# Two cross attentions of a four-layer kernel, from passes over pairs of batches to a pipeline over single batches

## The reference

```
# first layer, per batch; n = layernorm(x), c = ctx, all 256 x 256
q = n @ Wq + bq;  k = c @ Wk + bk;  v = c @ Wv + bv
x = x + tanh(g[0]) * softmax(q @ k.T / 16) @ v

# fourth layer, per batch, 16 heads of 16 features
q = elu(n @ Wq + bq) + 1;  k = elu(c @ Wk + bk) + 1;  v = c @ Wv + bv
S   = einsum('bhle,bhld->bhed', k, q)          # 16 x 16 per head
out = einsum('bhme,bhed->bhmd', v, S) / (sum over head of q*k + 1e-6)
x = x + tanh(g[3]) * (out @ Wo + bo)
```

## Time and profile before

| | |
|---|---|
| median of three runs | 3446.64 us |
| profiled execution, its own time | 3447.9 us |
| its span, from first to last instruction | 3446.2 us |
| PE busy | 3111.9 us, 90% |
| DVE busy | 1781.4 us, 52% |
| ACT busy | 1166.4 us, 34% |
| POOL busy | 355.1 us, 10% |
| mean granted clock of PE | 0.94 |

### The profile page before, as it was taken

How to read it: one execution, slowest core, us unless ns; L and a number is a source line. 1 busy time by engine, 2 the same in 40 slices (tenths; PEclk the granted TensorE clock), 3 DMA queues, 4 the chain that set the end, 5 groups by cost and what they waited for, 6 DMA issues and landing times. The chain is left out here.

```text
span 3446.2 us, 58510 instructions
## 1 busy us (share of the span) xinstructions
PE 3111.9 (90%) x21570; PEld 2500.1 (73%) x21571; DVE 1781.4 (52%) x4412; ACT 1166.4 (34%) x2167; POOL 355.1 (10%) x647
## 2 busy tenths in 40 slices
PE   7868999999997998997999979999799987774998
PEld 5755666666665887886888866666588866673998
DVE  4436777777772113774556557777323336651111
ACT  1213555555552112441212204555432222222221
POOL 1101111111100000000000000010001101113111
PEclk9888999999997999998999989999899988866999
DMA  3010000000002441001000000000111100054554
GB/s 108 0 31 1 1 0 0 0 0 0 0 1 74 151 153 45 18 18 47 0 0 0 0 27 1 0 0 0 57 50 49 49 17 0 0 160 141 182 179 132
DMA packets 93088, 145.92 MB, mean 42 GB/s; under 512 B 12878, under 2 KB 74574, under 8 KB 86864
## 3 DMA queue, kind: packets, MB, share of 16 engines
q1 hardware_dynamic: 89600, 136.39, 12.7%
q0 software_dynamic: 3408, 8.46, 0.7%
HBM read 131.18 MB, written 14.56 MB: 42 GB/s over the span
## 5 line engine op out<-in xcount | busy, mean ns | idle before, releaser
L464 DVE TENSOR_REDUCE m0hnm<-banks 128x4 f32<-128x1024 f32 x256 | 313.0, 1223 | 173.4 <-PE banks L392 173.3
L491 ACT ACTIVATE m0hpT<-banks 128x1024 f32<-128x1024 f32 x256 | 262.8, 1027 | 355.8 <-PE banks L405 355.8
L392 PE MATMUL banks<-m0hk,m0hq 32*128 32x256 f32 x2048 | 292.2, 403 | 12.6 <-DVE m0hnm L464 12.2
L405 PE MATMUL banks<-m0hq,m0hk 32*128 32x256 f32 x2048 | 291.6, 401 | 1.1 <-ACT m0hpT L491 1.1
L489 ACT ACTIVATE a2hpT<-banks,a2hlow 128x512 f32<-128x512 f32 x256 | 161.9, 684 | 181.5 <-PE banks L405 181.5
L392 PEld LDWEIGHTS banks<-m0hk,m0hq 32*128 32x128 f32 x2048 | 175.8, 185 | 64.7 <-DVE m0hnm L464 33.4
L464 DVE TENSOR_REDUCE a2hnm<-banks 128x4 f32<-128x1024 f32 x128 | 156.8, 1225 | 95.4 <-PE banks L392 95.1
L405 PEld LDWEIGHTS banks<-m0hq,m0hk 32*128 32x128 f32 x2048 | 177.7, 184 | 2.1 <-issue 1.7
L1579 ACT ACTIVATE E1sg<-banks 128x256 f32<-128x256 f32 x160 | 61.3, 383 | 326.4 <-PE banks L1596 326.4
L1596 PE MATMUL banks<-e1xnT,E1wg 128*128 128x256 f32 x640 | 166.1, 382 | 0.0
L1596 PE MATMUL banks<-e1xnT,E1wu 128*128 128x256 f32 x640 | 165.1, 381 | 0.0
(11 more groups left out here) (399 smaller groups left out, 6318.2 us busy)
## 6 DMA issues: line engine op xcount, KB each, us to landing
E3w<-in_L_ffn_W_dram SPq DMA_DIRECT2D x47, 1024.0 KB, 5.2
E0w<-in_L_ffn_fw_dram SPq DMA_DIRECT2D x64, 512.0 KB, 4.5
E2w<-in_L_ffn_w_dram SPq DMA_DIRECT2D x16, 1024.0 KB, 7.3
slots_x<-E3zeros SPq DMA_DIRECT2D x1, 5070.0 KB, 25.5
E3xin<-slots_x SPq DMA_DIRECT2D x39, 130.0 KB, 2.1
ctx_in<-in_ctx_dram SPq DMA_DIRECT2D x16, 256.0 KB, 4.8
x_all<-in_x_dram SPq DMA_DIRECT2D x16, 256.0 KB, 5.2
A1ctx_in<-in_ctx_dram SPq DMA_DIRECT2D x16, 256.0 KB, 2.7
```

Of the source, the lines that this page charges most:

```text
L392: ins = pe.matmul(self.scores[:, j, tc], self.q[strip(half, j), u, e, c, chunk(tc)], self.k[strip(half, j), u, e, c], start=True, stop=True)
L405: ins = pe.matmul(self.turned[:, j, kc], self.k[strip(half, j), u2, e2, c2, chunk(kc)], self.q[strip(half, j), u2, e2, c2], start=True, st ...
L464: v.tensor_reduce(self.nm[:, e, :, at:at + 33:32].rearrange("p c g -> p g c"), self.scores, AX.X, ALU.max, negate=True).then_inc(self.nm_r ...
L491: ins = a.activation(dst, self.turned, ACT.Exp)
```

## The change

Both stages run over single batches now. A slot `b` does the second half of batch `b` and the first half of batch `n = b + 1`, on the two sets of four banks in turn (`u` for b, `nu` for n); each engine's program names its steps for both in one order. The slots -1, 0 and 1 are written out, slots 2 to 11 run in a loop of five rounds of two (`Fori` leaves out its upper bound, as in `passes`), and slots 12 to 15 are written out behind it.

The layer norm is in a class `BatchFront`. Statistics and normalised rows are made three batches ahead (b + 3), the transposes of the normalised rows two ahead (b + 2). POOL's root and its copy of the context for batch b + 3 wait until PE is done with v of batch n.

- First attention, PE in a slot: q, k, v (n); transposes of `xn` (b + 2); transposes of the probabilities (b); scores (n); product with v (b). DVE: x of b - 1; q (n); reciprocal (b); statistics (b + 3); v (n); normalised rows (b + 3); maximum (n). ACT: k (n); `xnT` (b + 2); `prT` (b); Exp (n).
- Fourth attention, PE in a slot: q (n); product of k and q (b); k (n); product with v (b); v (n); transposes of `on` (b); transposes of `xn` (b + 2); product with Wo (b), now into bank T3. DVE: bias and x of b - 1; q (n); mask (b); statistics (b + 3); k (n); division (b); normalised rows (b + 3); sum of maximum and Exp, and denominator (n). ACT: Relu and Exp (n); `onT` (b); `xnT` (b + 2); v (n).
- The minimum on DVE is replaced by a Relu with scale -1 on ACT, followed by Exp with scale -1.
- The load of Wq and bq counts on a semaphore of its own (`q_in`), so q of the first batch waits for these two alone.

```diff
+def slots(eng, slot):
+    for b in (-1, 0, 1):
+        slot(b, b % 2)
+    with eng.Fori(1, 6) as i:
+        for u in (0, 1):
+            slot(2 * i + u, u)
+    for b in range(12, B):
+        slot(b, b % 2)
+
+class BatchFront:
...
+    def root(self, g, b, u):
+        g.wait_ge(self.mv_rdy, b + 1)
+        g.tensor_tensor(self.rstd[:, u], self.mv[:, u, :, 1], self.env.eps5[:], ALU.add).then_inc(self.var_rdy, 1)
+        g.wait_ge(self.var_rdy, b + 1)
+        g.tensor_tensor(self.rstd[:, u], self.rstd[:, u], self.env.mhalf[:, 0:C], ALU.pow).then_inc(self.rstd_rdy, 1)
+        g.tensor_copy(self.cT[:, u], self.env.ctxT[:, b]).then_inc(self.cT_rdy, 1)
...
 # both stages, POOL
+            def slot(b, u):
+                if live(b + 3):
+                    g.wait_ge(v_mm, b + 2)
+                    fr.root(g, b + 3, 1 - u)
...
 # layer0_attention, PE
+            def slot(b, u):
+                n, nu = b + 1, 1 - u
+                if live(n):
+                    pe.wait_ge(fr.xnT_rdy, n + 1)
+                    product(pe, lambda m: bankB[nu][:, m], lambda k, m: wq[:, k, chunk(m)],
+                            lambda k: fr.xnT[:, nu, k]).then_inc(q_mm, 1)
...
+                if live(b + 2):
+                    if live(b):
+                        pe.wait_ge(v_rdy, b + 1)
+                    fr.turn(pe, b + 2, u)
+                if live(b):
+                    pe.wait_ge(p_rdy, b + 1)
+                    transpose4(pe, bankC[u], pr[:, u], env.ident[:]).then_inc(pT_mm, 1)
+                if live(n):
+                    pe.wait_ge(q_rdy, n + 1)
+                    pe.wait_ge(k_rdy, n + 1)
+                    product(pe, lambda m: bankB[nu][:, m], lambda k, m: qT[:, nu, k, chunk(m)],
+                            lambda k: kT[:, nu, k]).then_inc(s_mm, 1)
+                if live(b):
+                    pe.wait_ge(v_rdy, b + 1)
+                    pe.wait_ge(pT_rdy, b + 1)
+                    pe.wait_ge(o_used, b + 1)
+                    product(pe, lambda m: bankD[u][:, m], lambda k, m: prT[:, u, k, chunk(m)],
+                            lambda k: vt[:, u, k]).then_inc(o_mm, 1)
...
 # layer3_attention, DVE
+            def slot(b, u):
+                n, nu = b + 1, 1 - u
+                if live(b - 1):
+                    add_up(b - 1, nu)
+                if live(n):
+                    v.wait_ge(q_mm, n + 1)
...
+                if live(b):
+                    v.wait_ge(den_rdy, b + 1)
+                    v.wait_ge(o_mm, b + 1)
+                    v.tensor_tensor(on[:, u].rearrange("p c (h k) -> p (c h) k", k=KD),
...
+                if live(b + 3):
+                    fr.normalised(v, b + 3, nu)
+                if live(n):
+                    v.wait_ge(ex_rdy, n + 1)
+                    v.scalar_tensor_tensor(qk[:, nu], qk[:, nu], 0.0, ex[:, nu], ALU.max, ALU.add).then_inc(qk_rdy, 1)
...
 # layer3_attention, ACT
+                if live(n):
+                    a.wait_ge(raw_rdy, n + 1)
+                    a.activation(ex[:, nu], qk[:, nu], ACT.Relu, scale=-1.0).then_inc(neg_rdy, 1)
+                    a.wait_ge(neg_rdy, n + 1)
+                    a.activation(ex[:, nu], ex[:, nu], ACT.Exp, scale=-1.0).then_inc(ex_rdy, 1)
```

More of the change, by code:

```diff
@@ L225, in _ @@
-            passes(g, body)
+            fr.root(g, 0, 0)
+            fr.root(g, 1, 1)
+            def slot(b, u):
+                if live(b + 3):
+                    g.wait_ge(v_mm, b + 2)
+                    fr.root(g, b + 3, 1 - u)
+            slots(g, slot)
         @block.vector
         def _(v):
[L229 to L244, removed]
+            v.sem_inc(o_used, 2)
+            fr.stats(v, 0, 0)
+            fr.stats(v, 1, 1)
+            fr.normalised(v, 0, 0)
+            fr.normalised(v, 1, 1)
+            v.wait_ge(q_in, 32)
+            def add_up(b, u):
+                v.wait_ge(ri_rdy, b + 1)
+                v.wait_ge(o_mm, b + 1)
+                for c in range(C):
+                    last = v.scalar_tensor_tensor(env.x[:, b, c], bankD[u][:, c], ri[:, u, c:c + 1], env.x[:, b, c],
+                                                  ALU.mult, ALU.add)
+                last.then_inc(o_used, 1)
@@ L269, in _ @@
-            passes(v, body)
+                if live(b + 3):
+                    fr.normalised(v, b + 3, nu)
+                if live(n):
+                    v.wait_ge(s_mm, n + 1)
+                    v.tensor_reduce(nm[:, nu, :], bankB[nu], AX.X, ALU.max, negate=True).then_inc(nm_rdy, 1)
+            slots(v, slot)
+            add_up(B - 1, (B - 1) % 2)
         @block.scalar
         def _(a):
[L273 to L282, removed]
+            fr.turned(a, 0, 0)
+            a.wait_ge(w_in, 64)
+            def slot(b, u):
+                n, nu = b + 1, 1 - u
+                if live(n):
+                    a.wait_ge(k_mm, n + 1)
                     for c in range(C):
-                        last = a.activation(kT[:, u, c], bankC[u][:, c], ACT.Identity, bias=bk[:, c:c + 1])
+                        last = a.activation(kT[:, nu, c], bankC[nu][:, c], ACT.Identity, bias=bk[:, c:c + 1])
@@ L291, in body @@
                     last.then_inc(p_rdy, 1)
[L292 to L297, removed]
+            slots(a, slot)
         @block.tensor
         def _(pe):
[L301 to L304, removed]
@@ L2224, in body @@
                     for c in range(C):
-                        last = a.activation(vT[:, u, c], T3[u][:, c], ACT.Identity, bias=bv[:, c:c + 1])
+                        last = a.activation(vT[:, nu, c], T3[nu][:, c], ACT.Identity, bias=bv[:, c:c + 1])
                     last.then_inc(v_rdy, 1)
-                for u in (0, 1):
-                    a.wait_ge(mn_rdy, nth(i, u))
-                    a.activation(ex[:, u], ex[:, u], ACT.Exp).then_inc(ex_rdy, 1)
-                if more:
-                    fr.scalar(a, i + 1)
```

340 lines of the change are left out of this document (175 added, 165 removed).

## The result

Four runs of the changed kernel took 3327.49 to 3338.82 us, median 3331.54; four of the kernel before, on the same chip, had a median of 3446.05. The ratio is 0.9674, with an interval of 0.9651 to 0.9697. Predicted were 3339 us and a range of 3318 to 3372. The profiled execution of the changed kernel took 3338.82 us (span 3337.1), the longest of the four. I work with its span first, because the prediction was made from a span too; the last experiment deals with the median. One run further down, of the kernel with the fourth attention alone changed, took 4532.94 us at a mean granted clock of 0.66, against 0.95 in the other three; no figure here counts it.

The account below looks back on a forecast made before the run. PE, the fullest engine, was taken to lose time to waits and the low clock in both stretches. Gains of 50.3 and 59.2 us, 109.5 together, took 3447.9 to 3338.4, given as 3339 us for the median, range 3318 to 3372.

Parts of the forecast that it names:

- the claim that every wait is covered: First attention: every cover is at least 0.8 us longer than what it hides, so PE bounds at 9.5 us a batch.
- the ring: Fourth attention: one slot's steps through DVE, PE and GpSimd, each released by the one before, take 11.0 us.
- chain to the reciprocal: Fourth attention, DVE: from the rectifier's sum to the reciprocal, 3.3 us a batch.
- The first chain: Start of the fourth attention: the first `qk` chain is done at 2816.4, with k(0) taking 2.3 us.
- The last, uncovered slot: End of the fourth attention: the last batch's steps, with nothing to hide them, take 8.9 us.
- Clock partly low: Fourth attention: clock stays partly low, about 12.0 us a slot, 16 us more, 3355; chance 0.09.
- Table loads: Fourth attention: Relu and Exp change tables, two loads a slot, ring 12.7, 27 us more, 3366; chance 0.04.
- The old wait: Fourth attention: the waits from before survive, 3.5 us a batch, slot 13.0, 32 us more, 3371; chance 0.04.
- The root off the ring: Fourth attention: GpSimd's root falls out of the ring, PE's 9.5 us bound, about 3317; chance 0.06.
- PE at 1.2 GHz throughout: Fourth attention: PE stays at the low clock, 19.0 us a slot instead of 11.0, total 3466; chance 0.03.
- The contention rule: Fourth attention: GpSimd's late copy could slow DVE's rectifier sum by up to 0.6 us, slot 11.6, total 3348.
- The sum of 109.5 us: Whole kernel: gains of 50.3 us in the first attention and 59.2 us in the fourth, taken together.

Follow-up runs that it names:

- the last experiment: Changed kernel unedited once more, then with four and with eight useless products at the end of its first attention: 3330.66, 3336.16 and 3344.43 us.
- the run with the loaded first attention: Changed kernel with six useless bn_stats a slot on DVE ahead of the statistics in the first attention: 3326.75 us.
- the free root: Changed kernel with POOL's root in the fourth attention no longer waiting for v(n), only its copy of the context: 3319.84 us, ratio 0.9648.

## Why the prediction was right, and where it was off

**First attention.** Slots of 9.51 us (q products at 45.31, 54.82, 64.33, 73.84), 9.5 predicted; q(0) at 36.36 (36.2), k(0) at 39.69 (39.6), the last sum done at 192.1 (191.8). The price of each step at the high level was read off the rows of before, and the claim that every wait is covered held.

**Fourth attention, the ring.** Term by term, from the slot shown above:

| step | predicted | measured |
|---|---|---|
| y and its sum | 1.66 | 1.52 (2841.62 to 2843.14) |
| bias of q | 0.79 | 0.67 |
| `sm` and the hand-over | 0.50 | 0.53 |
| o(b) on PE | 0.86 | 1.00 |
| v(n) | 1.73 | 1.73, and |
| hand-over to POOL | 0.2 | 0.32 (2847.07 to 2847.39) |
| root | 1.0 | 1.00 |
| normalisation beside one copy | 1.0 | 0.92 to the next start, 0.99 busy |
| chain to the reciprocal | 3.3 | 3.17 (2838.45 to 2841.62) |
| slot | 11.04 | 10.86, next one 11.13 |

The two terms that no row of before showed, POOL's wake-up by PE and the normalisation beside one copy, were sized right to 0.12 and 0.08. DVE's wait for the root came to 1.93 us, where I had 1.4: the stretch around it is 0.35 longer (o, the wake-up, the hand-over of `sm`), and statistics, bias k and `on` fill 2.27 of it and not 2.44. In every other slot y starts 0.47 us behind the reciprocal's start and not 0.26, and these are the slots of 11.13 us. They are slots 4, 6, 8 and 10, the first of each round of the loop but the round by which it is entered; in slots 2 and 12, where DVE enters and leaves the loop, it is 0.27. So the 0.2 us go with the way back at the loop's end, a term that the prediction's ring does not have; the other 0.07 stay open.

**What was off** in the stage is at its two ends, and cancels. The first chain was done 19.5 us after the stage's start, not 18.3: k(0) took 2.95 us where I had put 2.3. The fifteen slots took 161.5 us where I had 163. (As the terms are written, the prediction's sum ends at 2988.3, not at 2988.7.) The last, uncovered slot took 10.8 us and not 8.9. I had priced its PE steps at the high level, though PE stands idle three times in it; in the timeline:

```profile
2928.18 1.16 PE L2322 MATMUL banks<-A3sm,A3vT 128*128 128x128 f32 x8 [1.50 <-DVE A3sm L2231]
...
2931.70 3.78 PE L61 MATMUL banks<-A3wo,A3onT 128*128 128x256 f32 x8 [0.69 <-ACT A3onT L2283]
```

The last product took 3.78 us, the price of 1.2 GHz, 1.9 more than its 1.89. That is not fixed either: of the eleven profiles with a changed fourth attention five have 3.78 there and six 1.99, behind much the same idle times. In the run with the loaded first attention, one of the six, the last slot took 8.9 us, as predicted:

```profile
2922.82 1.99 PE L61 MATMUL banks<-A3wo,A3onT 128*128 128x256 f32 x8 [0.69 <-ACT A3onT L2287]
```

**The rivals.** *Clock partly low*: at the stage's start and end, but not in the loop, where PE's idle times are 0.3 to 0.5 us: 0.83, 1.00 and 0.69 in three stretches of the stage. The prediction's reason against it was in part wrong: before the change the clock did not stay up behind the stretch that the earlier trace rows show (1.00 from 2840 to 2850, 0.64 from 2850 to 2860).

```profile
2745.00:2786.00 41.00, 32.86 (x150) 0.83 0.13 36
2786.00:2926.00 140.00, 129.76 (x724) 1.00 0.00 0
2926.00:2938.00 12.00, 6.44 (x27) 0.69 0.00 0
```

*Table loads*: one in the stage, against the two a slot of the rival, between the first Relu and the first Exp. ACT's timeline:

```profile
2758.07 1.06 ACT L2278 ACTIVATE A3ex<-A3qk 128x1024 f32<-128x1024 f32 x1 [7.77 <-DVE A3qk L2242]
2759.15 1.28 ACT L2280 ACT_TABLE_LOAD   x1
2760.44 1.06 ACT L2280 ACTIVATE A3ex<-A3ex 128x1024 f32<-128x1024 f32 x1
```

The first Relu ran under the table that the stage before had left, and later ones under Exp's. By the Trainium skill ("ScalarE: Activation LUTs", Table sets), relu lies in every set; the trace agrees. The seven loads of the earlier trace rows, one for each pass of the old loop, are now this one, in the straight code ahead of the loop; why the old loop repeated its load no run shows. Relu took 1.06 us, as Exp does (1.0 predicted). *The old wait*: no wait for `qk` is left. *The root off the ring*: not so here, and built on purpose it gave 10.08 a slot and not PE's 9.5, since the price of PE's slot had left out the wait for `onT` (0.42) and what goes with it; my 3317 for it was 3 us short of the measured 3319.84. *PE at 1.2 GHz throughout*: nothing of it.

**The contention rule.** In the fourth attention DVE's sum of the rectifier, which reads two tensors in SBUF, takes 1.21 us when POOL is quiet and 1.39 when the free root moves POOL's copy beside it; the normalisation goes from 0.99 to 0.73 in exchange. Groups by line of the two kernels, changed first (busy us, mean ns of one):

```profile
L2255 DVE SCALAR_TENSOR_TENSOR A3qk<-A3qk,A3ex 128x1024 f32<-128x1024 f32 x15 | 18.2, 1213 | 2.3 <-ACT A3ex L2280 2.3
...
L101 DVE TENSOR_SCALAR a3xn<-x_all,a3mv,a3rstd 128x256 f32 x20 | 9.9, 535 | 19.2 <-POOL a3rstd L215 19.2
```

```profile
L2256 DVE SCALAR_TENSOR_TENSOR A3qk<-A3qk,A3ex 128x1024 f32<-128x1024 f32 x15 | 21.0, 1398 | 11.8 <-ACT A3ex L2281 11.8
...
L101 DVE TENSOR_SCALAR a3xn<-x_all,a3mv,a3rstd 128x256 f32 x20 | 7.3, 406 | 0.0
```

The Trainium skill ("GPSIMD Engine Reference", section 8, Key points) says that GpSimd shares its SBUF interfaces with VectorE, and contends with instructions in a two-port mode or with two SBUF inputs. The sum has two SBUF inputs, and the runs agree, at 0.18 us and not the 0.6 that I had allowed for. The normalisation's 0.26 us are of the same kind, but no run shows in which mode it runs. In the changed kernel itself the copy is over (2848.91) before the sum starts (2849.31), so the ring paid nothing for this.

**The median.** The sum of 109.5 us met the span's 109.1, in part by luck: the two stages gave 107.7, and the untouched ones happened to be shorter in this run. Yet the median, 3331.5, came out 7.5 us under my 3339. The step that failed is the last one: I turned the profiled execution into the median by what the kernel before had shown (1.3 us above its median) and rounded up. The changed kernel's profiled run lay 7.3 us above its median. In a second profile, of a run at its median, the stages are 163.2 and 192.6 us long, and the whole difference, 8.4 us, is in the middle, which the change doesn't touch. The prediction had put a change of the middle at nothing; its spread over the profiles, 2543.5 to 2555.2 us, is wider than the errors of all the other terms together.

## What to carry to other kernels

Once waits of PE are covered, look for a ring through the other engines: write down, for one slot, what each step is released by, until a step comes round again; put useless work on it and beside it to see whether it is the bound. An instruction that waits for a buffer it doesn't itself need, such as the root that shared its gate with the copy, is the first thing to take off the ring (11 us here, by one moved wait). Once the ring is open, look again at PE's own steps before the next move: here a wait of 0.42 us for a copy with too little cover made the slot, and work on DVE's order gained nothing. Don't put a fall of PE's busy time down to the clock alone: here 20 us of it were 14 of the clock and 12 of time.

## What was not expected of the hardware

- Useless PE work made the kernel before faster: 28 us of it in the first attention kept the granted clock at 1.00 (0.91 without), and the stage became 8.4 us shorter.
- The same untouched code took 2543.5 to 2555.2 us, with a granted clock of 0.81 to 0.90 in one stretch of 100 us; the changed kernel's own two profiles have the two ends, 0.81 and 0.90. One and the same last product took 1.99 or 3.78 us.
- The same `bn_stats` pair cost 0.05 or 0.67 us a slot by its place alone.
- DVE started the first step of a loop's round 0.2 us late (0.47 against 0.27), in four slots of each of seven profiles, and not where it entered or left the loop.
